# Eleven idle TensorE products ahead of the picks of each edge group in an attention stage

## What is computed

```
hn = batch_norm(h);  Q, K, V = hn @ Wq, hn @ Wk, hn @ Wv      # per head: 16 channels
score = clip(sum(K[src] * Q[dst]) / sqrt(16), -5, 5)          # per edge and head
a = exp(score - smax[dst]);  a = a / segment_sum(a, dst)[dst]
wV = segment_sum(V[src] * a, dst)                             # back to 3125 nodes
h2 = h + wV @ Wo + bo;  then a batch norm and two dense layers
```

## Time and profile before

| | |
|---|---|
| time, median of 3 runs | 1550.61 us (1548.57 to 1550.96) |
| the profiled execution | 1552.32 us |
| its span, first to last instruction | 1550.5 us |
| mean granted TensorE clock | 0.868 of full speed |
| TensorE busy | 1188.4 us, 77% |
| VectorE busy | 784.2 us, 51% |
| ScalarE busy | 435.1 us, 28% |
| GpSimd busy | 412.4 us, 27% |
| stage with the edge groups | from about 680 to 1382 us |

### The profile page before, as it was taken

How to read it: one execution, slowest core, us unless ns; L and a number is a source line. 1 busy time by engine, 2 the same in 40 slices (tenths; PEclk the granted TensorE clock), 3 DMA queues, 4 the chain that set the end, 5 groups by cost and what they waited for, 6 DMA issues and landing times. The chain is left out here.

```text
span 1550.5 us, 21379 instructions
## 1 busy us (share of the span) xinstructions
PE 1188.4 (77%) x7734; PEld 888.0 (57%) x7734; DVE 784.2 (51%) x1938; ACT 435.1 (28%) x862; POOL 412.4 (27%) x490
## 2 busy tenths in 40 slices
PE   2599999999999979554666676756677766767795
PEld 1477745555565535454666665756677666755453
DVE  4867736644345655633544444444454444545333
ACT  0566612112111111231332332323233332325111
POOL 3000000000000000135555555555555555610000
PEclk9977689999999999776788788878888877879998
DMA  5000060000000000053222222222222222218100
GB/s 145 12 1 1 1 204 7 8 0 1 7 1 20 17 21 1 21 167 84 76 79 78 76 82 82 79 72 82 82 73 84 79 82 79 85 31 182 25 20 22
DMA packets 49802, 88.01 MB, mean 57 GB/s; under 512 B 12429, under 2 KB 35488, under 8 KB 49459
## 3 DMA queue, kind: packets, MB, share of 16 engines
q0 software_dynamic: 20608, 55.20, 12.5%
q1 hardware_dynamic: 26610, 29.96, 7.2%
q10 hardware_dynamic: 2492, 1.61, 0.4%
HBM read 70.74 MB, written 15.98 MB: 56 GB/s over the span
## 5 line engine op out<-in xcount | busy, mean ns | idle before, releaser
L1342 POOL DMA_INDIRECT counts_all<-kv_d,counts_all x416 | 394.6, 948 | 314.4 <-DVE counts_all L1406 170.7
L830 PE MATMUL bank<-counts_all,parts 125*128 (+2 forms) x2100 | 412.2, 355 | 26.3 <-DVE parts L1021 9.8
L1457 PE MATMUL bank<-counts_all 125*128 125x128 f32 x1384 | 227.4, 329 | 197.2 <-ACT counts_all L1500 165.2
L1457 PEld LDWEIGHTS bank<-counts_all 125*128 125x128 f32 x1384 | 208.8, 237 | 211.0 <-ACT counts_all L1500 176.3
L830 PEld LDWEIGHTS bank<-counts_all,parts 125*128 125x128 f16 x2100 | 191.7, 98 | 231.3 <-issue 18.4
L1406 DVE TENSOR_TENSOR counts_all<-counts_all,bank 128x512 f32<-128x512 f32 x104 | 71.3, 685 | 244.1 <-ACT counts_all L1526 177.1
L1500 ACT CAST counts_all<-bank 125x1024 f32<-125x1024 f16 (+1 forms) x104 | 90.1, 866 | 289.4 <-remote 179.6
L1241 POOL IOTA iota_n<- 128x250 f16 x1 | 0.3, 346 | 588.9 <-POOLq L814 588.9
L1395 DVE TENSOR_TENSOR counts_all<-counts_all,bank 128x512 f32<-128x512 f32 x104 | 71.2, 684 | 124.0 <-remote 78.6
L1468 PE MATMUL bank<-counts_all,oh 128*125 128x136 f32 x696 | 109.2, 305 | 17.5 <-issue 15.7
L1468 PEld LDWEIGHTS bank<-counts_all,oh 128*125 128x125 f32 x696 | 98.2, 209 | 20.8 <-issue 18.8
(11 more groups left out here) (215 smaller groups left out, 1240.5 us busy)
## 6 DMA issues: line engine op xcount, KB each, us to landing
counts_d<-counts_all SPq DMA_DIRECT2D x1, 6835.9 KB
counts_all<-kv_d,counts_all POOLq DMA_INDIRECT x416
counts_all<-counts_d SPq DMA_DIRECT2D x1, 6152.3 KB
kv_d<-counts_all SPq DMA_DIRECT2D x6, 448.0 KB
q_d<-counts_all SPq DMA_DIRECT2D x1, 1562.5 KB
x<-in_x SPq DMA_DIRECT2D x6, 250.0 KB
out<-z SPq DMA_DIRECT2D x6, 250.0 KB
inv_deg<-in_x SPq DMA_DIRECT2D x1, 1400.0 KB
```

The source lines that it names most:

```text
L830: last = T.matmul(agg_ps[p][:, 0:w], pin[:, s, part, :], counts[:, s, bass.ds(b * BLK, w)], start=(s + part == 0), stop=(s + part == NT))
L1342: G.indirect_dma_start(out=out_rows, out_offset=None, in_=table_d, in_offset=bass.IndirectOffsetOnAxis(ap=index, axis=0)).then_inc(signal, 16)
L1457: last = T.matmul(ps[2 + n % 2][:, k * C:(k + 1) * C], ohT[n % 2][:, w, k, :], Q[:, GTILES[n][w], :], start=(w == 0), stop=(w == nw - 1))
```

## The change

In `pick(n)`, after the two waits and ahead of the products with Q, TensorE gets eleven products of `ident_h` (128 by 128, fp16) with `iota_n` (128 rows of 250 numbers, fp16). They go in turn to columns 0 to 249 and 256 to 505 of the bank that the picks of the group then write with `start=True`, so nothing of them is left. Nothing reads them and they carry no semaphore of their own.

```diff
@@ pick(n), L1452 ff. @@
                         if n >= 2:
                             pe.wait_ge(prod_ready, n - 1)
                         nw = len(GTILES[n])
+                        for i in range(11):
+                            T.matmul(ps[2 + n % 2][:, (i % 2) * 256:(i % 2) * 256 + 250], ident_h[:, :], iota_n[:, 0:2 * TILE], start=True, stop=True)
                         for k in range(GRP):
                             for w in range(nw):
                                 last = T.matmul(ps[2 + n % 2][:, k * C:(k + 1) * C], ohT[n % 2][:, w, k, :], Q[:, GTILES[n][w], :],
```

## The result

| | before | changed |
|---|---|---|
| median of 3 runs | 1550.61 us | 1593.88 us (1586.35 to 1608.82) |
| profiled execution | 1552.32 us | 1608.82 us |
| its span | 1550.5 us | 1607.0 us |

The ratio is 1.030, with a 95% interval of 1.018 to 1.042: slower, by 43 us where some 100 were forecast (1594 against 1651). The profiled execution is the slowest of the three, so its rows explain 56 us, 15 us more than the run in the middle lost.

The account below looks back on a forecast made before the run. Waits were taken to bound the gather stage, shown in GpSimd's 170.7 us wait for L1406 above its issue floor. Array time of 79 us plus 20 us for late completions, on 1552 us, gave 1651 us; range 1550 to 1745 us.

Parts of the forecast that it names:

- What bounds: Gather stage: waits set the pace above GpSimd's issue floor of 4.93 us a group; TensorE's completions come late during gathers.
- The bare price: On TensorE, eleven products of 250 columns take 1.22 us at full clock, 2.44 us at half.
- First term: Loop of copy, picks and turn: the products' array time is paid in 47 rounds, 79 us (zero to 175).
- Second term: Late rounds while gathers run: eleven more completions a group must come out, 20 us (nothing to 57).
- Rival (a): TensorE in the gather stage: added work keeps the clock up, 1535 us, or 1478 if the ring hides the products; chance 0.14.
- Rival (b): GpSimd's gathers: every group ends in a pause, 53 more of 3.5 us, 186 us, giving 1738 us; chance 0.18.
- Rival (c): TensorE's idle time and the ring's slack hide the products, or they cost far less; 1552 to 1560 us; chance 0.09.

Follow-up runs that it names:

- e13: The changed kernel run again, on a chip where the kernel before takes 1378 us: 1377.4 us, ratio 0.9995.
- e11: The kernel before with only the first four groups' gathers, on a chip where it takes 1544.2 us with all gathers: 1252.1 us.
- e2: The changed kernel with the same 2750 columns in six idle products instead of eleven: 1563.8 us, ratio 1.015 to the kernel before.
- e3: The changed kernel with the same 2750 columns in 22 idle products of 125: 1625.7 us, ratio 1.053 to the kernel before.
- e9: The changed kernel run again, on a chip where the kernel before takes 1544 us: 1586.4 us, ratio 1.028.
- e1: The changed kernel with its eleven idle products 16 columns wide instead of 250: 1565.1 us, ratio 1.017 to the kernel before.
- e10: The kernel before plus 22 idle products of 125 columns, on a chip where the kernel before takes 1544 us: 1623.7 us, ratio 1.049.
- e12: The kernel before with GpSimd allowed three groups ahead instead of four: 1543.5 us, ratio 1.000.
- e5: The kernel before with only the first four groups' gathers, on a chip where it takes 1378 us with all gathers: 1244.3 us.
- e15: 22 idle products of 125 columns with only the first four groups' gathers, where the kernel before takes 1378 us: 1360.4 us.
- e14: The changed kernel with only the first four groups' gathers, on a chip where the kernel before takes 1378 us: 1352.6 us.
- e7: 22 idle products of 125 columns with only the first four groups' gathers, in an earlier set (kernel before: 1378 us): 1361.7 us.
- e6: The changed kernel with only the first four groups' gathers, in an earlier set (kernel before: 1378 us): 1349.9 us.

## Why the prediction was right or wrong

**What bounds.** Right. The floor of GpSimd's issue, 4.93 us a group, is where the kernel runs when nothing is late: 5.0 us in e13. That gathers make TensorE's completions come out slowly, which was read out of the earlier trace rows, is shown by e11 for this kind of chip. That they are counted by product, an inference there, is borne out so far as more products (each with its load of weights) mean more late waits and more time.

**The bare price.** Right: 1.17 and 2.27 us for 1.22 and 2.44.

**First term, 79 us for array time on the loop.** Wrong, and this is the step that made the forecast twice the loss. The wait did grow as forecast, the copy's wait for the turn by 72 us. But a wait that grows is not yet time. Six, eleven and 22 products of the same 2750 columns cost 1.5%, 2.8 to 3.0% and 4.9 to 5.3%. A line through e2 and e3, which ran in one set, is (5.26 - 1.54) / 16 = 0.23% a product, and leaves 0.15%, some 2 us, for none; the intervals of the two leave about 13 us either way. Judged the other way, at a count of eleven, 250 columns (2.8% in e9) against 16 (1.7% in e1) are 1.1%, some 17 us, for 1.17 - 0.29 = 0.88 us of array time a group, so 23 us for all of it, though from two sets. And e2, whose late waits are no longer than before while the copy waits 123.1 us for the turn, loses 24 us in all. So the array time costs between 2 and some 24 us, not 79. This is net of what the products give back by holding the clock up (below), which the sum left out. Why it is so little was in part in the page: a round with late completions ends when they come out, and what TensorE does ahead of that is hidden in the lateness. The remote waits of the widening, some 150 us before and 30 after, are cover of this kind used up; they fall as the loss grows in the other runs too, 118 us in e2, 67 in e9, 9 and 7 in e3 and e10. That this is where the 79 us went is argued from these rows; no run isolates it.

**Second term, 20 us for the count.** Right in kind, and at the low end of what the runs give. In e1 eleven products with 0.29 us of array time cost 1.7%, 26 us; less their share of array time by the step above (1.1% x 0.29 / 0.88 = 0.4%) this leaves 20 us. By the 0.23% a product of e2 and e3 eleven are 2.6%, 40 us. No single line of number and array time goes through e1, e2 and e3, so the price of one product isn't a constant, and the runs give no more than a span from 20 to 40 us. The choice of the lower half rested on the backlog's ending with each burst. That reason doesn't hold: in the round of the earlier trace rows VectorE and ScalarE are released at 1037.36 and 1041.62 while the gathers go on,

```profile
1036.72 0.95 POOL L1342 DMA_INDIRECT counts_all<-kv_d,counts_all  x1 [1.17 <-issue]
...
1040.72 0.95 POOL L1342 DMA_INDIRECT counts_all<-kv_d,counts_all  x1 [0.30 <-issue]
```

and in e12 GpSimd may run less far ahead and nothing changes. The upper bound, 57 us for a third more products, is above the whole loss. The 0.36 to 0.53 us a product stand for a round in which gathers run throughout, and most of it never becomes time: 0.23% a product is 0.035 us a group.

**Rival (a), the clock.** It happened in part. The clock rose from 0.81 to 0.87. The mean record of a pick is 329 ns before and 304 ns after; it is 275 ns at full clock and 421 at half, so the share at half clock fell from 37% to 20%. At (3.78 - 2.05) / 16 = 0.11 us each this is 1384 x 0.17 x 0.11 = 26 us less of TensorE's time for the picks, an estimate; how much of it lies on the path, no run tells. It did not turn the sign, since the stalls stayed: the longest wait ahead of the products is 16.5 us. The rule cited from the Trainium skill (TensorE: Matmul & The Clock Gate, section "What's actually happening") agrees with the trace, 0.81 before and 0.87 with the added activity; it promises nothing on time, and here the products that held the clock up cost more time than it gave.

**Rival (b).** Wrong: 68 pauses of GpSimd in the stage instead of 49, not about 100. **Rival (c)** is wrong on the chip of the record; on that of e13 its outcome came, a change that costs nothing. It was argued from the idle time of TensorE; what decides is whether GpSimd's issue binds.

**Late completions lie outside the records.** In the earlier trace rows the turn ends at 1003.62 and is known to ScalarE at 1014.9. The Trainium skill (Perfetto Trace Analysis, section "Per-instruction lifecycle: what the profiler-reported window actually captures") says that the propagation of a semaphore falls outside an instruction's window. The trace agrees: up to 8.65 us of idling at ScalarE in these rows, and in e11 none once the gathers are over.

No version here is faster than the kernel before on a chip with late completions. e12 is its equal; all idle products are slower.

## What to carry to other kernels

Compare a consumer's start with the recorded end of what it waits for: where "remote" or "issue" stands for many microseconds, the producer's busy time is no measure of its cost, and what counts may be how many instructions it has. When adding a term to such a stage, ask which row becomes time (here GpSimd's wait for the ring) and scale that one; the growth of another wait is not a sum. And time a change on more than one chip: the same idle products cost 3% on one and nothing on another. A time expected ahead of a run should be given as a ratio to the kernel before on the same chip.

## What the runs showed of the hardware that was not expected

- The same kernel takes 1378 us on two chips and 1543 to 1551 us on the others. In the stage with gathers, 102 groups take 510 us on the first (with the change) and 680 us on the second (before).
- On the slower kind, TensorE's completions reach the other engines late while indirect DMAs from GpSimd run, with 11.3 us between the turn's recorded end and the copy's start in the earlier trace rows. Without the gathers such a chip takes 1252 us (e11), one of the other kind 1244 us (e5). What in the chip holds them back, no run shows.
- There idle products cost by their number: cutting the same 2750 columns into 22 instead of six costs 57 us by the ratios (3.7% of 1543 us), some 3.6 us for one more in each of 104 groups, where the array time grows by 5 us in all. Without gathers, 22 instead of eleven cost 8 and 12 us (e15 over e14, e7 over e6), with them 37 us.
- Eleven products of 16 columns, 0.29 us of array time a group, cost 1.7%; six products with 1.16 us cost 1.5%.
